# Cross-attention of a perceiver layer: the row of maxima made on VectorE by 32x32 turns, and a block's first scores joined with a pending weighing

## The reference

```python
q = _split_heads(x @ Wq)          # x: 16 x 64 x 512, 16 heads of 32
k = _split_heads(y @ Wk)          # y (context): 16 x 1601 x 512
v = _split_heads(y @ Wv)
attn = jnp.einsum('bhid,bhjd->bhij', q, k) * SCALE
attn = jax.nn.softmax(attn, axis=-1)
out = jnp.einsum('bhij,bhjd->bhid', attn, v)
return out.transpose(0, 2, 1, 3).reshape(b, n, h * d) @ Wp + bp
```

## Time and profile before

| | |
|---|---|
| median of 3 runs | 1843.1 us (1842.24 to 1843.58) |
| profiled execution | 1845.33 us |
| its span | 1843.4 us, mean granted TensorE clock 0.997 |
| TensorE busy (matmul) | 1821.4 us, 99% |
| TensorE weight loads | 1588.2 us, 86% |
| VectorE | 1133.7 us, 62% |
| ScalarE | 842.2 us, 46% |
| GpSimd | 904.1 us, 49% |
| DMA | 101.18 MB, mean 55 GB/s |

### The profile page before, as it was taken

The page is one execution under the profiler, slowest core; times in us unless marked ns, Lnnn a source line. Parts: engine busy times, 40 slices in busy tenths (PEclk is TensorE's granted clock), DMA queues, the critical chain, the costliest instruction groups (busy, mean ns, idle before and its releaser), DMA issues. The chain is left out here.

```text
span 1843.4 us, 65602 instructions
## 1 busy us (share of the span) xinstructions
PE 1821.4 (99%) x28988; PEld 1588.2 (86%) x28988; DVE 1133.7 (62%) x1366; ACT 842.2 (46%) x1046; POOL 904.1 (49%) x830
## 2 busy tenths in 40 slices
PE   8999999999999999999999999999999999999998
PEld 7979898989898989898989898988898877787887
DVE  6654848484747474757575666656575767574265
ACT  4634545454545454545444444544454533334332
POOL 0334727383838383828273737464645573434111
PEclk9999999999999999999999999999999999999999
DMA  6210202020202020202020202020111122023110
GB/s 240 119 53 2 83 3 82 3 82 4 82 4 82 4 82 3 82 4 82 3 82 4 82 3 82 9 77 19 66 40 45 55 100 90 23 92 103 47 58 23
DMA packets 43358, 101.18 MB, mean 55 GB/s; under 512 B 19121, under 2 KB 20657, under 8 KB 42961
## 3 DMA queue, kind: packets, MB, share of 16 engines
q1 hardware_dynamic: 43088, 96.88, 14.9%
HBM read 86.48 MB, written 8.29 MB: 51 GB/s over the span
## 5 line engine op out<-in xcount | busy, mean ns | idle before, releaser
L553 POOL TENSOR_TENSOR fold<-fold,prob 128x256 f32<-128x256 f32 (+1 forms) x704 | 723.1, 1027 | 55.2
L111 PE MATMUL ring<-y_parts,w_keep 128*128 128x402 f32 (+1 forms) x3072 | 607.6, 351 | 1.6 <-PEq L189 1.4
L111 PEld LDWEIGHTS ring<-y_parts,w_keep 128*128 128x128 f32 x3072 | 551.4, 188 | 16.1 <-issue 2.8
L111 PE MATMUL ring<-wv_s,y_parts 128*128 128x512 f32 x2304 | 552.2, 396 | 0.0
L111 PEld LDWEIGHTS ring<-wv_s,y_parts 128*128 128x128 f32 x2304 | 427.8, 188 | 95.4
L547 POOL TENSOR_TENSOR fold<-prob 128x256 f32<-128x256 f32 x64 | 68.2, 1066 | 656.1 <-ACT prob L608 656.1
L573 ACT ACTIVATE k_sb<-ring 128x402 f32<-128x402 f32 (+1 forms) x256 | 129.5, 506 | 362.6 <-PE ring L111 362.6
L753 DVE TENSOR_TENSOR prob<-prob,peak_rows 128x1024 f32<-128x1024 f32 (+1 forms) x192 | 275.2, 1486 | 13.4 <-ACT peak_rows L604 13.4
L598 ACT ACTIVATE prob<-s_ps 128x1536 f32<-128x1536 f32 (+1 forms) x128 | 200.0, 1562 | 132.2 <-PE s_ps L903 132.2
L608 ACT ACTIVATE prob<-prob 128x1024 f32<-128x1024 f32 (+1 forms) x192 | 207.5, 1123 | 4.7 <-DVE prob L753 2.9
L730 DVE TENSOR_TENSOR fold<-prob 128x512 f32<-128x512 f32 x64 | 50.9, 796 | 212.5 <-ACT prob L598 212.5
(11 more groups left out here) (212 smaller groups left out, 1580.3 us busy)
## 6 DMA issues: line engine op xcount, KB each, us to landing
y_raw<-yT SPq DMA_DIRECT2D x48, 804.0 KB, 6.5
y_raw<-yT SPq DMA_DIRECT2D x16, 792.0 KB, 9.2
f_raw<-w_ffn SPq DMA_DIRECT2D x22, 512.0 KB, 3.5
v_sb<-y_left SPq DMA_DIRECT2D x1, 2304.0 KB, 11.3
v_sb<-v_left SPq DMA_DIRECT2D x16, 130.0 KB
p_x<-x SPq DMA_DIRECT2D x4, 512.0 KB, 6.6
q_scratch<-p_x SPq DMA_DIRECT2D x8, 256.0 KB, 2.0
q_sb<-q_scratch SPq DMA_DIRECT2D x16, 128.0 KB, 8.8
```

Source lines behind the costliest of these rows:

```text
L111: mm = pe.matmul(out, left(a, c), right(b, c), start=(c == 0 and n == 0), stop=(c == DC - 1 and n == 2))
L553: pool.tensor_tensor(acc[0:m], acc[0:m], prob[0:m, i, t, :], ALU.add).then_inc(sum_step, 1)
```

## The change

VectorE makes the row of maxima by itself. It turns fold[:, i] in 32x32 blocks, reduces each block, brings the four quarters of the partitions to the first 32, reduces again, copies the result back to the other three quarters, and turns it, broadcast, into peak_rows. TensorE's turn and spread_peaks and ScalarE's peak_row go, with their waits. TensorE's order changes: a block's first half of scores stands directly before a weighing of the batch before, and block 2's second half of scores moves in among the values. ScalarE's and VectorE's orders follow. The prologue makes 56 warm-up transposes in place of 48.

```diff
-        WARM = 48
+        WARM = 56
@@ VectorE
-            def peaks(b, i):
+            def row_of_peaks(b, i):
                 block = NBLK * b + i
-                dve.wait_ge(turn_ok, block + 1)
-                dve.tensor_reduce(peak[:], turned.rearrange("p (k j) -> p k j", k=2), AX.X,
-                                  ALU.max).then_inc(peak_ok, 1)
+                step = ROW_N * block
+                first = slice(0, SQ)
+                others = [(k, slice(k * SQ, (k + 1) * SQ)) for k in range(1, P // SQ)]
+                dve.wait_ge(tree, TREE_N * (block + 1))
+                dve.transpose(peak_rows[:], fold[:, i, :]).then_inc(fold_read, 1)
+                dve.wait_ge(fold_read, block + 1)
+                dve.tensor_reduce(quarters[:, 0, :], peak_rows[:].rearrange("p (j q) -> p j q", q=SQ), AX.X,
+                                  ALU.max).then_inc(row_step, 1)
+                dve.wait_ge(row_step, step + 1)
+                for k, rows in others:
+                    dve.tensor_copy(quarters[first, k, :], quarters[rows, 0, :]).then_inc(row_step, 1)
+                dve.wait_ge(row_step, step + 4)
+                dve.tensor_reduce(peak[first, :], quarters[first].rearrange("p k j -> p j k"), AX.X,
+                                  ALU.max).then_inc(row_step, 1)
+                dve.wait_ge(row_step, step + 5)
+                for k, rows in others:
+                    dve.tensor_copy(peak[rows, :], peak[first, :]).then_inc(row_step, 1)
+                dve.wait_ge(row_step, step + 8)
+                dve.transpose(peak_rows[:].rearrange("p (j q) -> p j q", q=SQ),
+                              peak[:].unsqueeze(2).broadcast_to((P, HQ // SQ, SQ))).then_inc(row_step, 1)
@@ VectorE, keys_phase
-                largest(b, 0, 0)
-                if past:
-                    output(b - 1, 1)
-                largest(b, 0, 1)
-                for i in (1, 2):
-                    peaks(b, i - 1)
+                for i in (0, 1):
                     largest(b, i, 0)
-                    if not past and i == 2:
+                    if past:
+                        output(b - 1, i + 1)
+                    elif i == 1:
                         for j in range(LEFT_SLOTS):
                             left_low(j)
-                    subtract(b, i - 1)
                     largest(b, i, 1)
-                    if past:
-                        output(b - 1, i + 1)
+                    row_of_peaks(b, i)
+                    subtract(b, i)
+                largest(b, 2, 0)
+                if past:
+                    output(b - 1, 3)
@@ VectorE, values_phase
                 value(b, 0)
-                peaks(b, 2)
+                largest(b, 2, 1)
+                value(b, 2)
+                row_of_peaks(b, 2)
+                subtract(b, 2)
                 largest(b, 3, 0)
-                subtract(b, 2)
-                value(b, 2)
+                value(b, 4)
                 largest(b, 3, 1)
-                value(b, 4)
+                row_of_peaks(b, 3)
+                subtract(b, 3)
                 if more:
                     low(b + 1, 0)
-                peaks(b, 3)
                 value(b, 6)
-                subtract(b, 3)
                 value(b, 8)
@@ ScalarE, values_phase
+                score(b, 2, 1)
+                value(b, 1)
                 score(b, 3, 0)
-                value(b, 1)
-                peak_row(b, 2)
+                value(b, 3)
                 score(b, 3, 1)
                 exponential(b, 2, 0)
                 exponential(b, 2, 1)
                 exponential(b, 2, 2)
-                value(b, 3)
                 if more:
                     high(b + 1, 0)
...
                 value(b, 5)
-                peak_row(b, 3)
@@ TensorE, batch
+                def joined(i):
+                    scores(b, i, 0)
+                    if past:
+                        small_read(b - 1, i)
+                        weigh(b - 1, i + 1)
+
                 keys(b, 0, 0)
                 keys(b, 0, 1)
                 if past:
-                    small_rows(b - 1, 3)
+                    small_read(b - 1, -1)
                     weigh(b - 1, 0)
                 keys(b, 0, 2)
                 keys(b, 0, 3)
                 keys(b, 1, 0)
-                scores(b, 0, 0)
+                joined(0)
                 keys(b, 1, 1)
+                keys(b, 1, 2)
                 scores(b, 0, 1)
...
+                keys(b, 2, 0)
+                keys(b, 2, 1)
+                joined(1)
+                keys(b, 2, 2)
+                keys(b, 2, 3)
+                scores(b, 1, 1)
+                keys(b, 3, 0)
+                keys(b, 3, 1)
+                keys(b, 3, 2)
+                joined(2)
+                keys(b, 3, 3)
...
                 values(b, 0)
-                scores(b, 3, 0)
+                scores(b, 2, 1)
...
                 values(b, 1)
+                values(b, 2)
+                scores(b, 3, 0)
+                values(b, 3)
+                values(b, 4)
                 scores(b, 3, 1)
-                for t in range(2 if past else 3, 6):
-                    values(b, t)
-                small_rows(b, 2)
-                turn(b, 3)
-                values(b, 6)
-                spread_peaks(b, 3)
-                for t in range(7, VT):
+                for t in range(5, VT):
                     values(b, t)
```

More of the change, by code:

```diff
@@ L47 @@
 TREE_N = 7
+SQ = 32
+ROW_N = 9
 PIECES = ((0, 4), (4, 8), (8, JT))
@@ L415, in cross_attention @@
         peak_rows = sb("peak_rows", [P, HQ])
-        peak = sb("peak", [P, 2])
+        quarters = sb("quarters", [P, P // SQ, HQ // SQ])
+        peak = sb("peak", [P, HQ // SQ])
         rec = sb("rec", [P, N])
@@ L420, in cross_attention @@
         small_ps = ctx.enter_context(nc.psum_tensor("small_ps", [P, 512], F32))
-        turned, spread = small_ps[:, 0:HQ], small_ps[:, HQ:2 * HQ]
         full, act_out, dve_out = sem("ring_full"), sem("ring_act_out"), sem("ring_dve_out")
         q_in, s_full, s_out = sem("q_in"), sem("s_full"), sem("s_out")
-        tree, turn_ok, peak_ok = sem("tree"), sem("turn_ok"), sem("peak_ok")
-        spread_ok, row_ok, sub_ok, exp_ok = sem("spread_ok"), sem("row_ok"), sem("sub_ok"), sem("exp_ok")
+        tree, fold_read, row_step = sem("tree"), sem("fold_read"), sem("row_step")
+        sub_ok, exp_ok = sem("sub_ok"), sem("exp_ok")
         sum_step, pv_ok, rec_ok, o_out, o_stored = (sem("sum_step"), sem("pv_ok"), sem("rec_ok"), sem("o_out"),
@@ L544, in totals @@
                 acc = fold[:, i, :]
-                pool.wait_ge(turn_ok, NBLK * b + i + 1)
+                pool.wait_ge(fold_read, NBLK * b + i + 1)
                 pool.wait_ge(exp_ok, done + 1)
@@ L600, in score @@
                                ACT.Copy).then_inc(s_out, 1)
-            def peak_row(b, i):
-                act.wait_ge(spread_ok, NBLK * b + i + 1)
-                act.activation(peak_rows[:], spread, ACT.Copy).then_inc(row_ok, 1)
             def exponential(b, i, n):
@@ L628, in keys_phase @@
                     value_weights()
[L629 to L642, removed]
-                    if not past and i == 2:
-                        for j in range(LEFT_SLOTS):
-                            left_high(j)
+                key(b, 1, 0)
+                score(b, 0, 0)
+                key(b, 1, 1)
+                key(b, 1, 2)
+                score(b, 0, 1)
+                key(b, 1, 3)
+                if not past:
+                    for j in range(LEFT_SLOTS):
+                        left_high(j)
+                key(b, 2, 0)
+                key(b, 2, 1)
+                score(b, 1, 0)
+                key(b, 2, 2)
+                exponential(b, 0, 0)
+                exponential(b, 0, 1)
+                key(b, 2, 3)
+                score(b, 1, 1)
+                exponential(b, 0, 2)
+                key(b, 3, 0)
+                key(b, 3, 1)
+                key(b, 3, 2)
+                score(b, 2, 0)
+                exponential(b, 1, 0)
+                exponential(b, 1, 1)
+                key(b, 3, 3)
+                exponential(b, 1, 2)
                 if not past:
@@ L905, in scores, with small_read @@
                 mm.then_inc(s_full, 1)
[L907 to L924, removed]
+            def small_read(b, i):
                 reached(pe, o_out, NBLK * b + i + 1)
@@ L983, in batch @@
                 values(b, 0)
-                scores(b, 3, 0)
[L985 to L988, removed]
+                scores(b, 2, 1)
+                if not past:
                     left_emptied(LT - 1)
                 values(b, 1)
[L991 to L995, removed]
-                scores(b, 3, 1)
-                for t in range(2 if past else 3, 6):
-                    values(b, t)
-                small_rows(b, 2)
-                turn(b, 3)
-                values(b, 6)
-                spread_peaks(b, 3)
-                for t in range(7, VT):
+                values(b, 2)
+                scores(b, 3, 0)
```

(4 more changed lines are left out.)

4 lines of the change are left out of this document (1 added, 3 removed).

## The result

The changed kernel takes 1968.74 us (median of 4 runs, 1966.92 to 1970.94) against 1842.67 us: ratio 1.0685, 95% interval 1.0666 to 1.0704. The profiled execution has a span of 1969.2 us. Forecast were 1911 us, with 1870 to 1952 as the range: the sign and the place of the loss are as forecast, its size is 126 us in place of 68, and the time lies outside the range.

The account below looks back on a forecast made before the run. TensorE's own list was taken to bound the kernel. Batches 1 to 14, 14 x (-2.3 + 5.5 + 1.4) = +64.4, batch 15 +2.8, batch 0 +1.8, prologue -0.8: +68 on 1843.1, 1911 us, range 1870 to 1952.

Parts of the forecast that it names:

- TensorE's list: TensorE's own work per batch: shrinks by 2.3 us, to 87.4 us if nothing waits.
- The wait's place and cause: Each batch, TensorE waits before value tile 9 for VectorE's copy of tile 6, now behind other VectorE work.
- The wait's size: TensorE could start tile 9 at S + 12.6, but the copy ends at S + 18.1: 5.5 us.
- S: Start of block 3's second half of scores on TensorE, now between value tiles 4 and 5.
- the row: VectorE's row of maxima, ten instructions: 2.6 us with GpSimd using the memory, bounds 2.0 and 4.2.
- low: VectorE's low(b+1, 0), ahead of the copy of tile 6: 1.8 us, ending at S + 17.4.
- dear row: Rival: VectorE's row of maxima takes 4.2 us, counted twice, so the wait is 8.7 us: 1962 us; chance 0.10.
- The clock: After each wait TensorE's clock falls to the 1.2 GHz level, costing 1.4 us more.
- the held products of batch 0: Left-over products in batch 0 are no longer held: their 2.0 us wait and its 1.4 us go.
- VectorE's chain runs quiet: Rival: GpSimd's sums fall elsewhere, wait 1.9 us: 1831 us, or 1803 with no wait; chance 0.12.
- No relief from the joins and the transposes: Rival: TensorE's list stays at 89.7 us, with the wait of 5.5 on top: 1947 us; chance 0.06.
- The clock stays up: Rival: the same wait, but TensorE's clock does not fall after it: 1889 us; chance 0.12.

Follow-up runs that it names:

- Experiment 1: Changed kernel with VectorE's copies of value tiles 6, 8 and 10 moved earlier, ahead of low(b+1, 0): 1815.16 us, ratio 0.9841 to the kernel before.
- Experiments 1 and 2: The second of these: changed kernel with only low(b+1, 0) moved from ahead of the copy of tile 6 to behind it: 1935.68 us.
- Experiment 3: Changed kernel with 64 unused transposes of the unit matrix on TensorE between value tiles 8 and 9 of each batch: 1984.20 us.
- Experiment 6: Changed kernel with GpSimd's softmax sums cut to 2 of 256 columns, number of adds and waits kept: 1867.46 us.
- experiments 7 and 9: The first of these: kernel before with its old orders, row of maxima made on VectorE, turns and spreads gone, 56 warm-up transposes: 1819.79 us, ratio 0.9873.
- experiments 1 and 9: The second of these: Experiment 1 with each pending weighing one unit of keys behind the scores instead of directly behind them: 1822.81 us.
- experiment 10: Changed kernel with the edits of Experiment 1 and experiment 5 together: 1814.80 us.
- experiment 5: Changed kernel with the six small copies of each row of maxima made as reductions over one element: 1931.19 us.
- experiment 8: Kernel before in its old orders with VectorE's row of maxima, plus first halves of scores of blocks 0 to 2 directly before pending weighings: 1827.77 us.
- experiment 4: Experiment 3 with the filler made of 29 products of 512 columns in place of 64 transposes: 2039.55 us.

## Why the prediction was wrong in its size

- **TensorE's list.** Forecast 2.3 us less a batch. Of the 97.90 us of the loop's mean batch, 7.90 are the wait and 2.31 the slow tiles; 87.7 are left, 2.1 less than before. Experiment 1, without the wait, repeats after 87.71. Right, 0.2 too high.
- **The wait's place and cause.** Right: once a batch, in front of tile 9, for the copy of tile 6. Experiments 1 and 2 show it by moving the copy and by taking one term out.
- **The wait's size.** This is the first step that failed: 5.5 us forecast, 7.9 measured. From S on: the maxima start at +3.5 (forecast +3.2); they take 4.9 us (4.66); the row 4.38 (2.6); the subtractions 4.87 (5.14); low 2.27 (1.8); copy and release of tile 6 0.73 (0.68). The sum is 20.7 for 18.1. The term that was mis-sized is the row: it makes 1.8 of these 2.6 us, low 0.5. (The maxima start late because VectorE, forecast to be free, is still copying tile 4 until 810.69.) Its transposes and reductions cost what I had put (0.45 and 0.42 us, beside GpSimd or not); the estimate of 0.62 us for a transpose was too high. The six small copies did not: three of them take 0.55 us quiet and 1.30 to 1.35 beside GpSimd. I had taken them from tiny operations of the prologue, where GpSimd is idle, and had added only 0.2 us for the contention, although showed two-input operations slowed beside it. The forecast's own bound of 4.2 us for a dear row, put down to the transposes and given 0.10, was nearer the truth for another reason. That its 1962 us lie near the measured time is luck: it counts the row's excess twice and so has 8.7 us of wait, where 7.9 were measured, and it has the forecast's 1.4 us for the clock.
- **low.** 1.82 us in the one instance that I looked at the earlier trace rows; here 2.35. The instance had GpSimd busy too; it was an instance and not the worst case.
- **The clock.** The second step that failed: 1.4 us forecast after each wait, from a wait of 2.0 us in batch 0; 1.5 to 3.0 measured after 7.9 us, 2.3 in the mean. In the batch shown the low level (1.2 GHz) holds over the whole of 827 to 833, three stretches of 2 us like the one in the earlier trace rows. Experiment 3 shows that the clock is the cause: with the wait filled, the same 36 matmuls take 8.45 us.
- **Together:** the waits are 123.2 us in place of 86.2 (14 x 5.5 + 5.5 + 3.7), 37 more; the slow clock 36.4 in place of 22.4, 14 more; TensorE's list 0.2 us in 16 batches, 3; the final weighings 3; and the prologue gave 0.7 more than put down. That is 57 us; the miss is 58. The wait's size is two thirds of it.
- **Elsewhere.** The prologue gained 1.5 us (keys begin at 38.89 in place of 40.41), where 0 to 1.6 had been forecast and 0.8 put down; the held products of batch 0 wait 0.2 us in place of 2.0. The keys stretch is free of waits, as forecast. 3.1 us of idle time in the final weighings were not forecast.
- **The rivals.** "VectorE's chain runs quiet" would have needed GpSimd's sums elsewhere. Experiment 6 makes it quiet, and even then 2.6 us of wait are left, and 25 us over the kernel before. "No relief from the joins and the transposes" is refuted by experiments 7 and 9. "The clock stays up" is refuted by the granted clock.
- **The Trainium skill** (TensorEngine Tiling, Key Properties: each change of tiling mode drains). The rule left the joins no gain; experiments 1 and 9 measure 7.7 us for them. A drain may be there at each border, but a join has one border less; no run shows the drain itself.

## What to carry to other kernels

Before moving work in an engine's list, follow the list down to the copy that frees a buffer of the bounding engine, and put that copy in front of the work that nobody waits for soon. Add up a chain that decides from durations taken beside the engines that will run at that moment, small operations above all, and count the slow clock after a long wait as part of the wait. Where such a chain holds small SBUF-to-SBUF copies on VectorE beside a busy GpSimd, try them as reductions over one element: here, with 8 numbers on 32 partitions, that took 38 us off; off the path (experiment 10) it gave nothing.

## What the runs showed of the hardware that was not expected

- VectorE's copy of 8 numbers on 32 partitions, SBUF to SBUF: 163 ns in the median, up to 620 ns with GpSimd busy (mean 319). The same as a reduction: 150 ns. A 32x32 block transpose of 128x256: 0.45 us and a reduction of it 0.42, both unmoved by GpSimd. The Trainium skill (VectorE: DVE Perf Modes, the perf-mode tier table) gives the copy a mode that uses both read ports and the reduction none, and (GPSIMD Engine Reference, Specifications) has GpSimd share its SBUF interfaces with VectorE instructions that use two; the trace agrees, and by these rules the edit of experiment 5 could have been foreseen.
- Idle times inside TensorE's small products that wait for nothing visible: 0.8 us, mostly once a batch, in experiment 8, up to 1.6 us three times a batch in experiment 3, and up to 3.2 us at the start of the loop's body in experiment 4; none in the loop of the changed kernel or of experiments 1, 7 and 9 between 200 and 1400 us. For one program they stay near one place of the list, and change with it. The traces hold one more thing: a DMA queue that the profile names "q8 instruction", with transfers of 16 KB of about 1 us. Each of the 118 idle times of over 0.5 us of this kind in experiments 3, 4 and 8 (120 to 1650 us) ends 1.2 to 1.7 us after such a transfer has ended; only 8% of all moments lie so behind one. So TensorE seems to have run out of instructions there. That is argued from the times and not shown: no experiment moved the transfers, and what makes them late in one program and not in another stays open.
- After each wait of 3.2 us or more for a copy of tile 6 the clock fell (experiments 2, 5 and the changed kernel); after waits of 2.5 to 2.6 us it fell 13 times in 15 (experiment 6), and after one of 0.8 us it did not. What it costs is not set by the wait's length alone: after equal waits of 7.90 us it was 1.5, 2.4 and 2.8 to 3.0 us in turn.
